# Second norm's transposes moved from TensorE to VectorE and DMA, and two-bank VectorE instructions, in an eight-layer linear-attention and expert kernel

## What is computed

```python
def layer(h):                                   # 8 layers, 16 heads of 8
    q, k, v = phi(h@wq+bq), phi(h@wk+bk), h@wv+bv        # phi = elu + 1
    kv = sum_s k_s v_s                          # per sequence of 256 and head
    att = q·kv / (q·sum_s k_s + 1e-6)
    h = LN(h + att@wo + bo, g1, be1)            # first norm
    y = gelu(h@w1 + c1) @ w2 + c2
    return LN(h + y, g2, be2)                   # second norm
x = x + LN(layers(LN(x)), gf, bef)
x = x + experts(LN(x))                          # 8 experts, top 2, weighted
```

## Time and profile before

| | |
|---|---|
| three runs | 1095.01, 1097.68, 1098.82 us; median 1097.68 us |
| span of the profiled execution | 1097.7 us |
| busy, share of span | TensorE 1017.6 us (93%), VectorE 790.8 (72%), ScalarE 834.7 (76%), GpSimd 767.4 (70%) |
| granted TensorE clock, mean | 0.970 |
| 32 slots of the layers | about 33 to 835 us of the span |
| experts' blocks and the end | about 835 to 1097 us |
| DMA | 85154 packets, 81.00 MB |

### The profile page before, as it was taken

How to read it: one execution, slowest core, us unless ns; L and a number is a source line. 1 busy time by engine, 2 the same in 40 slices (tenths; PEclk the granted TensorE clock), 3 DMA queues, 4 the chain that set the end, 5 groups by cost and what they waited for, 6 DMA issues and landing times.

```text
span 1097.7 us, 25115 instructions
## 1 busy us (share of the span) xinstructions
PE 1017.6 (93%) x7766; PEld 957.2 (87%) x7766; DVE 790.8 (72%) x2850; ACT 834.7 (76%) x1621; POOL 767.4 (70%) x1157
## 2 busy tenths in 40 slices
PE   5799899999999999999999999999999859889983
PEld 4798899999999999999999999999988749889983
DVE  6777677777777777777777777777788988933514
ACT  6777788888788888888888888888886746555572
POOL 5958877677767767776777677776675676757742
PEclk9999999999999999999999999999998969979997
DMA  4100010080008003500530075200000346557684
GB/s 136 50 1 16 20 50 2 15 164 15 1 19 165 11 1 68 115 12 15 96 83 1 16 129 139 40 1 2 1 1 1 99 144 185 148 164 217 203 256 149
DMA packets 85154, 81.00 MB, mean 74 GB/s; under 512 B 6780, under 2 KB 66179, under 8 KB 85024
## 3 DMA queue, kind: packets, MB, share of 16 engines
q1 hardware_dynamic: 80480, 70.93, 26.1%
q0 software_dynamic: 4544, 8.47, 2.2%
HBM read 44.82 MB, written 29.44 MB: 68 GB/s over the span
## 4 chain that ended last, share of the span: by engine, by line
PE 70%; DVE 9%; POOL 8%; issue 5%; ACT 3%; SPq 3%; DMA 2%; POOLq 0%; DVEq 0%
PE ps L1828 17%; PE ps L1705 8%; PE ps L1707 8%; PE ps L1706 8%; PE ps L1758 7%; PE ps L1752 5%; PE ps L1786 5%; PE ps L1985 4%; PE ps L1969 4%; PE ps L1740 2%; ACT s L948 1%; DVE x_lo L1233 1%; POOL xs L856 1%; POOL rstd L685 1%; DVE stat L1151 1%
## 5 line engine op out<-in xcount | busy, mean ns | idle before, releaser
L948 ACT ACTIVATE s<-s,shift,rstd 128x128 f32<-128x128 f32 x496 | 203.9, 485 | 50.1 <-POOL shift L687 48.9
L1828 PE MATMUL ps<-this_w,hid 128*128 128x128 f32 x1792 | 214.3, 275 | 0.0
L1828 PEld LDWEIGHTS ps<-this_w,hid 128*128 128x128 f32 x1792 | 206.9, 192 | 0.0
L932 ACT ACTIVATE hid<-ps,col 128x512 f32<-128x512 f32 x256 | 155.2, 684 | 2.4 <-PE ps L1707 2.1
L685 POOL TENSOR_TENSOR rstd<-var,neg_half 128x4 f32<-128x4 f32 x132 | 144.5, 1095 | 11.0
L728 POOL TENSOR_TENSOR res_a<-s,row 128x512 f32<-128x512 f32 x60 | 76.8, 1280 | 72.3 <-ACT s L948 67.5
L682 POOL TENSOR_SCALAR shift<-mv 128x4 f32<-128x4 f32 x132 | 26.9, 203 | 123.4 <-DVE mv L1155 123.3
L1151 DVE BATCH_NORM_STATS2 stat<-s 128x6 f32<-128x128 f32 x512 | 110.2, 276 | 0.0
L1705 PE MATMUL ps<-x_hi,this_w 128*128 128x512 f32 x224 | 95.3, 425 | 1.2 <-DVE x_lo L1233 1.2
L713 POOL TENSOR_TENSOR res_f<-res_f,row 128x512 f32<-128x512 f32 x64 | 92.1, 1438 | 5.0
L1985 PE MATMUL ps<-heads,hid 128*128 x624 | 87.3, 285 | 5.1 <-ACT hid L1077 4.5
(11 more groups left out here) (261 smaller groups left out, 2788.5 us busy)
## 6 DMA issues: line engine op xcount, KB each, us to landing
xs<-pad SPq DMA_DIRECT2D x6, 2925.0 KB, 18.0
res_a<-w SPq DMA_DIRECT2D x40, 256.0 KB
xblk<-xs SPq DMA_DIRECT2D x78, 65.0 KB
raw_w<-w SPq DMA_DIRECT2D x18, 256.0 KB, 7.3
row<-rows SPq DMA_DIRECT2D x8, 512.0 KB, 4.8
this_w<-next_w SPq DMA_DIRECT2D x7, 512.0 KB, 3.2
third_w<-w SPq DMA_DIRECT2D x10, 256.0 KB, 17.2
scaled_w<-w SPq DMA_DIRECT2D x10, 256.0 KB
```

Of the source, the lines that this page charges most:

```text
L932: a.activation(hid[h][:, c, :], ps(3 + h + c), ACT.Gelu, bias=col[:, bass.ds(lw * FF + (C_C1 + c), 1)]).then_inc(hid_done, 1)
L948: ins = a.activation(dst[:, t, :], src[:, t, :], ACT.Identity, bias=shift[i][:, t:t + 1], scale=rstd[i][:, t:t + 1])
L1828: ins = t_.matmul(ps(down_bank(l, s, h))[:, t * P:(t + 1) * P], hid[h][:, c, t * P:(t + 1) * P], down[:, c, :], start=c == 0, stop=c == FF ...
```

## The change

Of every pair whose next use lies at least four slots ahead (26 of the 28 pairs that are flipped after their second norm; the two others are neighbours of the exchange in `ORDER`) the second flip is done without TensorE:

- VectorE's `turn` transposes each 32×32 block of the normed half `s2[h]`, each at its own place in the grid, in one instruction per half, and writes them to `xrow[0]`, a buffer that only the experts' part uses. `turn(s-2,0)` stands before `lo_xt(s-2,0)`'s old place, `turn(s-2,1)` at the end of VectorE's slot, where `lo_xt(s-2,1)` stood.
- SyncE's `swap_blocks` then moves the blocks to their places: 16 DMAs, each from 32 partitions to 32 partitions, 8 runs of 32 floats (128 bytes) on each partition, into `feature`, which takes the place of the two buffers `xn_t`. They wait for both halves' `turn`.
- One slot later ScalarE's `split_moved` and VectorE's `lo_moved` do from `feature` what `split_xt` and `lo_xt` did from PSUM. Both halves now stand together, where `split_xt(·,0)` and `lo_xt(·,0)` stood.
- `turn(·,0)` waits until the 16 copies of the pair before have landed.
- TensorE leaves out `flip_x2` for these pairs, and `project` waits for no bank of theirs.
- `fill` is cut into three pieces per layer; the pieces and the copies are placed in SyncE's queue as the diff shows.
- The keys, the values and the attention rows are each written by one VectorE instruction of 512 columns across two banks. PSUM becomes one tensor for this.
- `wait_apart` becomes `wait`. With the constant counts that this kernel has, both issue the same instruction.

```diff
-FILL = XROWS // P // FILLS
+PIECES = 3
+FILL = XROWS // P // FILLS // PIECES
...
+def next_use(i):
+    k, p = ORDER[i]
+    return ORDER.index((k + 1, p))
+MOVED = [k < LAYERS - 1 and next_use(i) >= i + SLOTS for i, (k, _) in enumerate(ORDER)]
+FLIPPED = [k < LAYERS - 1 and not MOVED[i] for i, (k, _) in enumerate(ORDER)]
...
+        feature = sb("feature", [P, 2, N])
+        xn_t = [feature[:, k, :] for k in range(2)]
...
+        def turned(h):
+            return xrow[0][:, h, :, 0:P]
...
+            def swap_blocks(l, s):
+                if not swapped(l, s):
+                    return
+                sp.wait_ge(turned_done, moves_upto(l, s))
+                if any(MOVED[:l * SLOTS + s]):
+                    sp.wait_ge(xt_lo_done, flipped_upto(l, s, 0) - 1)
+                both = xrow[0][:, :, :, :].rearrange("p h t c -> p (h t) c")
+                for q in range(QUADRANTS):
+                    for f in range(QUADRANTS):
+                        sp.dma_start(
+                            feature[f * BLOCK:(f + 1) * BLOCK].rearrange("p h (t n) -> p (h t) n", n=P)
+                            [:, :, q * BLOCK:(q + 1) * BLOCK],
+                            both[q * BLOCK:(q + 1) * BLOCK, :, f * BLOCK:(f + 1) * BLOCK]).then_inc(swapped_in, 16)
...
             def layer(l, ring):
+                swap_blocks(l, -3)
                 load_raw(l + 1)
                 set_w1(l)
+                if l > 0:
+                    fill((l - 1) * PIECES * FILL)
+                swap_blocks(l, -2)
                 load_rows(l + 1, 1 - ring)
                 set_w2(l)
+                if l > 0:
+                    fill(((l - 1) * PIECES + 1) * FILL)
+                swap_blocks(l, -1)
+                if l > 0:
+                    fill(((l - 1) * PIECES + 2) * FILL)
+                swap_blocks(l, 0)
                 if l + 1 < LAST:
                     set_qkv(l + 1)
                 set_wo(l + 1)
...
+            def split_moved(l, s, h):
+                wait(act, swapped_in, 16 * QUADRANTS * QUADRANTS * (moves_upto(l, s) // 2))
+                wait(act, kvp_mm, upto(l, s, h))
+                a.activation(xt_hi[:, half_at(l, s, h)], feature[:, h, :], ACT.Copy).then_inc(xt_hi_done, 1)
...
-                flips = p2 and not final(l, s - 2)
+                flips = p2 and flipped(l, s - 2)
+                if swapped(l, s - 3):
+                    split_moved(l, s - 3, 0)
+                    split_moved(l, s - 3, 1)
                 if flips:
                     split_xt(l, s - 2, 0)
...
-                for half in two:
-                    b = (1, 4)[h] + half
-                    src = ps(b).rearrange("p (t n) -> p t n", t=2)
-                    ins = d.tensor_tensor(kt[h][:, 2 * half:2 * half + 2, :], src[:, :, 0:P],
-                                          row[:, ring, R_BK:R_BK + 1, :].to_broadcast([P, 2, P]), ALU.add)
-                ins.then_inc(kt_done, 1)
+                src = pair_tiles((1, 4)[h])
+                d.tensor_tensor(kt[h][:, :, :], src[:, :, 0:P],
+                                row[:, ring, R_BK:R_BK + 1, :].to_broadcast([P, T, P]), ALU.add).then_inc(kt_done, 1)
...
+            def lo_moved(l, s, h):
+                wait(dve, xt_hi_done, flipped_upto(l, s, h))
+                u = half_at(l, s, h)
+                d.tensor_tensor(xt_lo[:, u], feature[:, h, :], xt_hi[:, u].bitcast(F32),
+                                ALU.subtract).then_inc(xt_lo_done, 1)
+            def turn(l, s, h):
+                wait(dve, x2_done, upto(l, s, h, base=8))
+                wait(dve, swapped_in, 16 * QUADRANTS * QUADRANTS * (moves_upto(l, s) // 2 - 1))
+                d.transpose(turned(h), s2[h][:, :, :]).then_inc(turned_done, 1)
...
+                if turns:
+                    turn(l, s - 2, 0)
+                if swapped(l, s - 3):
+                    lo_moved(l, s - 3, 0)
+                    lo_moved(l, s - 3, 1)
                 if flips:
                     lo_xt(l, s - 2, 0)
                 if p1:
                     add_res2(l, s - 1, 0)
...
                 if flips:
                     lo_xt(l, s - 2, 1)
+                if turns:
+                    turn(l, s - 2, 1)
...
-                flips2 = p2 and not final(l, s - 2)
+                flips2 = p2 and flipped(l, s - 2)
```

More of the change, by code:

```diff
@@ L154, in input_upto, with swapped, flipped, moves_upto @@
     return flips_upto(ORDER.index((l - 1, p)), h) if l else 2 * p + h + 1
+def next_use(i):
[3 more added lines that the diff above has]
+FLIPPED = [k < LAYERS - 1 and not MOVED[i] for i, (k, _) in enumerate(ORDER)]
+BLOCK = 32
+QUADRANTS = P // BLOCK
+def swapped(l, s):
+    return l * SLOTS + s >= 0 and MOVED[l * SLOTS + s]
+def flipped(l, s):
+    return l * SLOTS + s >= 0 and FLIPPED[l * SLOTS + s]
+def moves_upto(l, s, h=1):
+    return 2 * sum(MOVED[:l * SLOTS + s]) + h + 1
+def pe_flips_upto(l, s, h):
+    return HALVES + 2 * sum(FLIPPED[:l * SLOTS + s]) + h + 1
 def banks_upto(l, s):
     i = l * SLOTS + s
-    while ORDER[i][0] == LAYERS - 1:
+    while i >= 0 and not FLIPPED[i]:
         i -= 1
-    return flips_upto(i, 1)
+    return flips_upto(i, 1) if i >= 0 else HALVES
 def build(nc, x, rows, cols, wqkv, wo, w1, w2, router, out):
@@ L427, in set_w1 @@
             def set_w1(l):
-                wait_apart(sp, w1_split, l * 8 + 8, sp_passed)
-                wait_apart(sp, w1_mm, upto(l, -1, 1, per=FF), sp_passed)
+                wait(sp, w1_split, l * 8 + 8)
+                wait(sp, w1_mm, upto(l, -1, 1, per=FF))
                 sp.dma_start(this_w1[:, :, :].bitcast(F32), next_w1[:, :, :].bitcast(F32)).then_inc(w1_in, 16)
@@ L472, in load_end_rows @@
                                  .partition_broadcast(P).unsqueeze(1)).then_inc(last_in, 16)
-            def fill(first):
-                if isinstance(first, int) and first == 0:
-                    sp.wait_ge(const_done, 1)
-                sp.dma_start(xs.rearrange("(n p) c -> p n c", p=P)[:, bass.ds(first, FILL)],
-                             pad[:, :, :].to_broadcast([P, FILL, XW])).then_inc(filled, 16)
             layer(0, 0)
@@ L930, in gelu @@
                         wait(act, w2_mm, upto(l, s - 1, h))
-                    wait_apart(act, w1_mm, upto(l, s, h, per=FF) - (FF - 1 - c), act_passed)
+                    wait(act, w1_mm, upto(l, s, h, per=FF) - (FF - 1 - c))
                     a.activation(hid[h][:, c, :], ps(3 + h + c), ACT.Gelu,
@@ L1152, in moments @@
                 ins.then_inc(stats, 1)
-                wait_apart(dve, stats, count, dve_passed)
+                wait(dve, stats, count)
                 for t in range(T):
@@ L1238, in add_res2 @@
                 wait(dve, resf_done, upto(l, s, h))
-                if l * SLOTS + s > 0 and not final(l, s - 1):
-                    wait(dve, t2_mm, flipped_upto(l, s - 1, h))
+                if flipped(l, s - 1):
+                    wait(dve, t2_mm, pe_flips_upto(l, s - 1, h))
+                elif swapped(l, s - 1):
+                    wait(dve, turned_done, moves_upto(l, s - 1, h))
                 if l == LAST and s == 3:
@@ L1385, in slot @@
                 p1, p2 = not first or s >= 1, not first or s >= 2
-                flips = p2 and not final(l, s - 2)
+                flips = p2 and flipped(l, s - 2)
+                turns = p2 and swapped(l, s - 2)
                 if begins_layer(l, s):
```

126 lines of the change are left out of this document (59 added, 67 removed).

## The result

The changed kernel takes 1077.26 us (median of 4 runs, 1076.00 to 1078.74), the kernel before 1096.35 (4 runs of the same comparison, 1094.38 to 1098.82). The ratio is 0.983, with a 95% interval of 0.981 to 0.985. The forecast was 1089.6 us.

What follows compares the result with a forecast made beforehand. TensorE was taken to bound the kernel, with 70% of the chain of waits. Per slot −0.44 (flip) − 0.07 (keys) + 0.20 (`lo_moved`) = −0.31 us; 26 slots, −8.1, took 1097.7 to 1089.6 us, range 1080 to 1108.

Steps and rivals of the forecast that it cites:

- The window and the half flip: One layer's window has TensorE busy 103.00 of 103.70 us; removing flip_x2(0) after attention(0) gains its 0.44 us in full.
- F: Piece of the slot worked out after the runs: attention(0) to the next ff_down(0) on TensorE, 6.30 us before, 5.86 after.
- VectorE isn't earlier: Without flip_x2(1), project(0)'s products come at 433.67, but VectorE starts the keys no sooner, turn(1) standing where lo_xt(1) stood.
- this half is lost: Removing flip_x2(1), ahead of project(0), gains none of its 0.44 us: TensorE reaches flip_x1(0) early and waits for ScalarE's norm.
- The stretch B: VectorE from add_res1(1) to the keys; the prediction took its 2.6 us as VectorE's own, not shortened by the flip's removal.
- D: Piece worked out after the runs: last step of moments1(s-1,1) to lo_x1(1), through GpSimd, ScalarE and VectorE; 8.27 before, 8.28 after.
- give nothing: Merging values and attention rows on VectorE saves no time: ScalarE's chain from phi_k(0) does not wait for values.
- C: Piece worked out after the runs: keys_values(0) to the last step of moments1(s-1,1) on VectorE; 2.23 us before, 2.06 after.
- `lo_moved` +0.20: VectorE before add_res2(0): lo_moved(0) is held by GpSimd's offset_resid(0) until 428.69, making add_res1(1) 0.2 us late per slot.
- The copies: SyncE's 16 DMAs of a pair land 13.2 us after turn(1), at 46 ns a run, before the next turn(0) needs them.
- rival B: Small things eat the gain: a slow turn, both lo_moved held, or set_w2 late over 50 ns a run; 1094 to 1101 us, chance 0.20.
- A: Rival: both flips' removal gains the whole 22.9 us, 1074.8 us, if VectorE's stretch to the keys shrinks 0.44 us; chance 0.07.

Runs made afterwards that it cites:

- run 2: Changed kernel with four dead transposing matmuls put back on TensorE where flip_x2(s-2,0) stood: 1091.21 us, ratio 0.996 to the kernel before.
- run 6: Changed kernel with turn(1) done twice, the first time into a buffer nobody reads: 1091.09 us (one run).
- run 8: Changed kernel with turn(1) moved later, behind the next slot's first keys and values: 1090.37 us, ratio 0.994 to the kernel before.
- run 4: Changed kernel with the keys alone written by two instructions again: 1081.34 us, ratio 0.990 to the kernel before.
- run 12: Changed kernel with keys, values and attention rows each written by two instructions again: 1082.14 us, ratio 0.988 to the kernel before.
- runs 1 and 9: Changed kernel, first with dead matmuls back where flip_x2(s-2,1) stood: 1085.78 us; then instead with turn(1) moved between add_res1(0) and add_res1(1): 1069.97 us.
- run 7: Changed kernel with each block copy cut in two, 32 DMAs of 64-byte runs instead of 16 of 128: 1220.17 us (one run).

## Why the prediction was wrong

**The window and the half flip, right.** TensorE was the place to look, and `flip_x2(0)`'s 0.44 us came in full: in F, and back when the flip came back (run 2).

**The failed step: "VectorE isn't earlier", "this half is lost".** Three things are wrong in it.
- The stretch B was not VectorE's 2.58 us. Its instructions start before the listed end of the one ahead. In the earlier trace rows `lo_xt(1)` starts at 433.42 and the keys at 434.20, 0.78 apart, where 0.60 does without a wait: VectorE was ready about 0.18 us early and waited for the products behind the flip. Taking the flip away gave 0.17 (B 2.58 to 2.41); putting it back took it again (2.59).
- TensorE's next wait was looked for at `flip_x1(0)`. There is one there, and later keys show at it (run 6). But `attention(0)` binds as well, behind a chain of constant length (D, 8.26 to 8.28 us in every row of the table) that starts at `moments1(s-1,1)`; what delays that costs time even where the keys come earlier (run 8). The one entry that TensorE had among its waits named that place, and I set it aside as 0.2 us.
- The values "give nothing": they stand ahead of `moments1(s-1,1)`, so their 0.07 us counts like the keys'. Of the 0.17 by which C fell, 0.13 are the merges: 0.06 the keys (run 4), forecast at 0.07, and 0.07 the values (run 12). The other 0.04 go with the keys' wait behind the flip: C is 2.10 where the keys wait for products again (runs 1 and 9). The attention rows give nothing, as forecast.

**The other failed step: `lo_moved` +0.20.** The contention is there; the profile after, source lines of `turn` and `lo_moved` (ns, min/median/max):

```profile
L1326 DVE STREAM_TRANSPOSE xrow<-s x52: 677/680/703, 85.7 to 759.4; 128x512 f32<-128x512 f32 x52
...
L1319 DVE TENSOR_TENSOR xt_lo<-feature,xt_hi x52: 676/752/1758, 114.6 to 779.0; 128x512 fp32r<-128x512 f32 x52
```

The two take 2.23 us beside GpSimd's residual rows, and still VectorE idles 0.20 us before `add_res1(1)`, as before. I let `lo_moved(0)` begin when GpSimd's row ends and added listed durations. It ends 0.55 us behind that row instead of 0.68 (426.67 and 426.12), and with starts some 0.08 us before the end ahead, the row of instructions from 425.04 is ready in time. The Trainium skill (SBUF — State Buffer, SBUF: two separate sides) has VectorE instructions with two SBUF inputs and GpSimd's that read SBUF exclude each other for a whole instruction. The trace agrees: `keys(1)` ends 0.54 to 0.55 us behind GpSimd's `res_f<-s,row` in the kernels before and after, whenever it began.

By the terms: 0.31 forecast, plus 0.20 that `lo_moved` did not cost, plus 0.21 of the flip (0.17 in B, 0.04 in C), plus 0.06 of the merges (0.13 for 0.07), is 0.78.

**The copies, right.** The profile after, DMA issues (KB each, us from issue to landing):

```profile
feature<-xrow SPq DMA_DIRECT2D x416, 32.0 KB, 2.0
...
this_w<-w SPq DMA_DIRECT2D x7, 256.0 KB, 5.5
```

Sixteen issues from 431.24, the last some 10.5 us later, and 2.0 to land: 12.5 us behind the end of `turn(1)`, where 13.2 was forecast, though by another bound: issuing costs 0.70 each, not 0.59, and the runs cost nothing beyond it. No `turn(0)` and no `split_moved` waits for them. `set_w2` was the tight one, as said: it lands in 5.5 instead of 2.8 us, and stalls once by 1.0 us. (The prediction's terms for its landing, 14.6 + 1.6 + 1.3, make t0 + 17.5 and not 18.3; of the forecasts only rival B's 50 ns and the 11 us at 57 ns rest on that.) The Trainium skill (DMA: Bandwidth & Descriptors, Specifications) has transfers under 512 bytes done by read-modify-write, and (Why small descriptors are slow (HBM only)) excepts SBUF to SBUF; run 7, with 64-byte runs landing in 1.9 us, agrees with the exception. The transposition took 0.68 us, forecast 0.66.

**The chances.** A had 0.07, on the ground that B would have to shrink by 0.44 us. That condition asked too much: the 0.78 us, short of A's 0.88 by 0.10, needed 0.17 from B. That the time came out near A's is partly chance: 0.65 of the 0.78 us are the flips' (0.44 and 0.21), and 0.13 are the merges', which A does not count.

**Still open.** That GpSimd's residual rows set D is read from the alignment of starts and ends in the traces; no run moved them alone. Why some early slots have a longer D is open. Whether ScalarE's passes would bind next is not known.

## What to carry to other kernels

Close the ring before pricing an edit: follow one slot from an instruction to the same one in the next slot, through every engine, and write the differences of starts, not durations, beside TensorE's own sum; the larger of the two is the slot, and an edit counts only where it lies on it. A small, regular wait (here 0.2 us before `attention(0)`) names the ring that holds the slot, or will when the bound engine gets faster. And when an instruction is moved to a busy engine, try its place: the same `turn(1)` cost 13 us in one and gained 7 in another.

## What the runs showed of the hardware that I had not expected

- VectorE instructions of 512 columns without a wait between them start 0.57 to 0.60 us apart, with listed durations of 0.65 to 0.70: a sum of durations overstates a row of them by some 0.08 us each.
- VectorE's transposition of 32×32 blocks, 128×512 float32, takes 0.68 us, no more than a pass that only adds.
- SBUF-to-SBUF copies of 32 partitions with 64-byte or 128-byte runs land in 1.9 to 2.0 us each, beside each other; the issue, 0.67 to 0.70 us a DMA, is what limits them.
